# Low parts of the up projection's weights: from VectorE's subtractions to accumulating transfers

## What is computed

```python
kernel = 2.0 * einsum('hn,hnl->hl', Cs, exp(P)).real      # one filter of 1024 taps per channel h
y = irfft(rfft(u * mask) * rfft(kernel))[..., :L] + u * mask * D
y = y * mask
# y as rows of 1024 (xf), 64 batches x 64 channels
scores = xf @ Wr.T                                        # 64 experts
top_vals, top_idx = top_k(scores, 16); gates = softmax(top_vals)
h = einsum('nd,krd->nkr', xf, A)                          # up: 1024 -> 64 experts x 16
out = einsum('nkr,kdr->nd', h * G[:, :, None], B) * 2.0   # down: 64 x 16 -> 1024
return x + out
```

## Time and profile before

| what | value |
|---|---|
| median of the runs | 894.25 us |
| the profiled execution | 894.25 us, its span 892.5 us |
| TensorE busy | 879.5 us, 99% of the span |
| VectorE busy | 753.8 us, 84% |
| ScalarE busy | 376.1 us, 42% |
| GpSimd busy | 6.5 us |
| DMA engines, mean busy share by slice of 22.3 us | 0.7, 0.7, 0.2, 0.1, 0.3, 0.1, then about 0.4 |
| one step of the loop | 26.7 us |

### The profile page before, as it was taken

How to read it: one execution, slowest core, us unless ns; L and a number is a source line. 1 busy time by engine, 2 the same in 40 slices (tenths; PEclk the granted TensorE clock), 3 DMA queues, 4 the chain that set the end, 5 groups by cost and what they waited for, 6 DMA issues and landing times.

```text
span 892.5 us, 15771 instructions
## 1 busy us (share of the span) xinstructions
PE 879.5 (99%) x4478; PEld 781.4 (88%) x4478; DVE 753.8 (84%) x2597; ACT 376.1 (42%) x642; POOL 6.5 (1%) x22
## 2 busy tenths in 40 slices
PE   5999999999999999999999999999999999999998
PEld 3667999998889998889999889999889999889997
DVE  8989998988889888889888889888889888888722
ACT  5763563444444344444344444334444334442100
POOL 2000000000000000000000000000000000000000
PEclk9999999999999999999999999999999999999999
DMA  7721315444333444333444434444333445333331
GB/s 238 241 57 47 77 33 141 141 118 121 115 120 108 124 118 126 115 119 111 118 118 131 113 117 110 118 118 137 110 116 108 118 118 141 111 114 114 93 95 48
DMA packets 74759, 103.32 MB, mean 116 GB/s; under 512 B 23972, under 2 KB 56804, under 8 KB 74740
## 3 DMA queue, kind: packets, MB, share of 16 engines
q1 hardware_dynamic: 74212, 102.63, 40.2%
q0 software_dynamic: 160, 0.10, 0.2%
q10 hardware_dynamic: 368, 0.36, 0.1%
HBM read 67.34 MB, written 34.93 MB: 115 GB/s over the span
## 4 chain that ended last, share of the span: by engine, by line
PE 95%; DVE 3%; ACT 1%; issue 0%; DMA 0%; ACTq 0%; DVEq 0%
PE out_ps L1432 26%; PE h_ps L1432 19%; PE out_ps L1436 13%; PE h_ps L1436 9%; PE turn_ps L1432 8%; PE turn_ps L1436 4%; PE conv_ps L1388 2%; PE conv_ps L1389 2%; PE conv_ps L1390 2%; PE conv_ps L1361 1%; PE conv_ps L1398 1%; PE conv_ps L1362 1%; PE conv_ps L1399 1%; PE conv_ps L1400 1%; PE conv_ps L1363 1%; PE h_ps L1441 1%
## 5 line engine op out<-in xcount | busy, mean ns | idle before, releaser
L1432 PE MATMUL out_ps<-b_lo,g_hi 128*128 128x512 f32 x496 | 196.1, 395 | 0.0
L1432 PE MATMUL out_ps<-b_hi,g_hi 128*128 128x512 f32 x496 | 194.7, 393 | 0.3 <-ACT g_hi L584 0.3
L1432 PE MATMUL h_ps<-a_hi,y_hi 128*128 128x384 f32 x480 | 161.4, 336 | 0.0
L1432 PE MATMUL h_ps<-a_lo,y_hi 128*128 128x384 f32 x480 | 161.3, 336 | 0.0
L1436 PE MATMUL out_ps<-b_hi,g_lo 128*128 128x512 f32 x496 | 122.6, 389 | 0.0
L1432 PEld LDWEIGHTS out_ps<-b_lo,g_hi 128*128 128x128 f32 x496 | 93.2, 188 | 21.2
L1432 PEld LDWEIGHTS out_ps<-b_hi,g_hi 128*128 128x128 f32 x496 | 93.0, 188 | 20.4 <-ACT g_hi L584 0.9
L1436 PEld LDWEIGHTS out_ps<-b_hi,g_lo 128*128 128x128 f32 x496 | 93.0, 188 | 20.0
L857 DVE SCALAR_TENSOR_TENSOR z<-swapped,step_other,part 128x64 f32<-128x64 f32 x384 | 92.3, 282 | 11.9
L850 DVE SCALAR_TENSOR_TENSOR part<-z,step_own,conv_ps 128x64 f32<-128x64 f32 x384 | 90.5, 277 | 8.7 <-ACT z L486 0.4
L1436 PE MATMUL h_ps<-a_hi,y_lo 128*128 128x384 f32 x480 | 93.1, 336 | 0.0
(11 more groups left out here) (244 smaller groups left out, 1480.7 us busy)
## 6 DMA issues: line engine op xcount, KB each, us to landing
xt_in<-in_xt SPq DMA_DIRECT2D x32, 512.0 KB, 3.3
x_in<-in_x SPq DMA_DIRECT2D x62, 256.0 KB, 3.7
out<-x_in SPq DMA_DIRECT2D x62, 256.0 KB, 3.1
moved<-square_sb SPq DMA_DIRECT2D x28, 512.0 KB, 2.7
square_sb<-moved SPq DMA_DIRECT2D x112, 128.0 KB, 2.9
b_in<-in_b_t SPq DMA_DIRECT2D x8, 512.0 KB, 7.8
a_in<-in_a_t SPq DMA_DIRECT2D x8, 512.0 KB, 9.1
moved_in<-square_in SPq DMA_DIRECT2D x26, 128.0 KB, 2.8
```

Source lines behind the costliest of these rows:

```text
L1432: pe.matmul(o, hi[:, c, :], moving[:, c, columns], start=first and c == order[0] and moving is w_hi, stop=False)
```

## The change

`low_up` is gone from VectorE. ScalarE writes the negative of the rounded high part over `a_in` (which is `a_lo`'s memory) in three calls, each for one third, and GpSimd issues transfers that add `a_t` and `wr_t` from memory to it: -a_hi + a = a_lo. The order is part 2, part 0 (two transfers), part 1. Part 2's columns are turned before tile 1 has used them, so tile 1's last third is multiplied from high and low parts; for that tile 1's `y` gets a high part (ScalarE) and a low part (VectorE), and the last four chunks of `a`'s columns 0 to 384 are rounded early in one call (`high_last`), the rest of these chunks in `split_rest`.

```diff
@@ gpsimd @@
+            pool.wait_ge(s_minus_hi, 1)
+            pool.dma_start(a_lo[:, :, 0:384], a_t[:, :, 0:384], accum_op=ALU.add).then_inc(s_alo[2], 16)
+            pool.wait_ge(s_minus_hi, 2)
+            pool.dma_start(a_lo[:, :, 768:ER], a_t[:, :, 768:ER], accum_op=ALU.add).then_inc(s_alo[0], 16)
+            pool.dma_start(a_lo[:, :, ER:EW], wr_t, accum_op=ALU.add).then_inc(s_alo[0], 16)
+            pool.wait_ge(s_minus_hi, 3)
+            pool.dma_start(a_lo[:, :, 384:768], a_t[:, :, 384:768], accum_op=ALU.add).then_inc(s_alo[1], 16)
@@ scalar @@
+            def high_last():
+
+                for i in LATE[5:]:
+                    act.wait_ge(s_w[i], 16)
+                act.activation(a_hi[:, NC // 2:NC, 0:384], a_in[:, NC // 2:NC, 0:384], ACT.Copy).then_inc(s_hilast, 1)
+
+            def split_rest(i):
+
+                _, arrived, hi, _ = loads[i]
+                act.activation(hi[:, 384:ER], arrived[:, 384:ER], ACT.Copy).then_inc(s_whi, 1)
+
+            def minus_high(n, up_before, highs):
+
+                _, c0, width, _ = H_PARTS[n]
+                act.wait_ge(s_up, up_before)
+                act.wait_ge(s_hilast, 1)
+                act.wait_ge(s_whi, highs)
+                act.activation(a_lo[:, :, c0:c0 + width], a_in[:, :, c0:c0 + width], ACT.Copy, scale=-1.0).then_inc(s_minus_hi, 1)
@@ scalar, first_step @@
                 decays(2)
+                high_last()
+                minus_high(2, 3, len(HIGH) - 4)
                 sines(2)
...
                 first_copies(2)
+                for i in range(HT):
+                    high_y(1, i)
                 tables(3)
                 for i in LATE[5:]:
-                    split_weights(i)
+                    split_rest(i)
@@ scalar, second_step @@
                 high_z(2)
+                minus_high(0, 4, len(HIGH))
                 high_turned(1, 0, 2, g_hi)
...
                 high_x(3)
+                minus_high(1, 5, len(HIGH))
                 copy_k(3)
@@ vector @@
-            def low_up(n):
-
-                _, c0, width, _ = H_PARTS[n]
-                columns = slice(c0, c0 + width)
-                dve.wait_ge(s_whi, len(HIGH))
-                dve.wait_ge(s_up, 3 + n + 1)
-                dve.tensor_tensor(out=a_lo[:, :, columns], in0=a_in[:, :, columns], in1=a_hi[:, :, columns].bitcast(F32),
-                                  op=ALU.subtract).then_inc(s_wlo, 1)
@@ vector, second_step @@
                 gate(1)
+
+                for i in range(HT):
+                    low_y(1, i)
                 states(2, range(MIDDLE, FED))
                 gates_of(1)
                 gate_part(1, 0)
-                low_up(0)
                 low_near(2)
...
-                low_up(1)
                 for i in range(HT):
                     low_y(2, i)
                 low_x(3)
-                low_up(2)
@@ tensor, up @@
-                    if first:
-                        pe.wait_ge(s_wlo, len(MIDST) + n + 1)
+                    if first and n < 2:
+                        pe.wait_ge(s_whi, len(HIGH))
+                        pe.wait_ge(s_alo[n], 16 * (2 - n))
@@ tensor, second_step @@
-                for n in range(len(H_PARTS)):
+                for n in range(2):
                     for c in range(NC):
                         last = whole_product(n, c)
                     last.then_inc(s_up, 1)
+
+                o, c0, width, _ = H_PARTS[2]
+                pe.wait_ge(s_yhi, HT)
+                pe.wait_ge(s_alo[2], 16)
+                product_high(o, y_hi, a_hi, a_lo, slice(c0, c0 + width), range(NC), first=True)
+                pe.wait_ge(s_ylo, HT)
+                product_low(o, y_lo, a_hi, slice(c0, c0 + width), range(NC)).then_inc(s_up, 1)
```

More of the change, by code:

```diff
@@ L207, in build @@
         s_whi, s_wlo = sem("s_whi"), sem("s_wlo")
+        s_hilast, s_minus_hi, s_alo = sem("s_hilast"), sem("s_minus_hi"), [sem(f"s_alo_{n}") for n in range(3)]
         s_theta, s_whole, s_args, s_sine, s_decay, s_powers, s_other, s_raw = (
@@ L878, in low_y @@
                 head = slice(i * B, (i + 1) * B)
-                dve.wait_ge(s_yhi, HT * (t - EXACT) + i + 1)
+                dve.wait_ge(s_yhi, HT * (t + 1 - EXACT) + i + 1)
                 dve.tensor_tensor(out=y_lo[:, :, head], in0=y_m[:, :, head], in1=y_hi[:, :, head].bitcast(F32),
                                   op=ALU.subtract).then_inc(s_ylo, 1)
-            def low_up(n):
-                _, c0, width, _ = H_PARTS[n]
-                columns = slice(c0, c0 + width)
-                dve.wait_ge(s_whi, len(HIGH))
-                dve.wait_ge(s_up, 3 + n + 1)
-                dve.tensor_tensor(out=a_lo[:, :, columns], in0=a_in[:, :, columns], in1=a_hi[:, :, columns].bitcast(F32),
-                                  op=ALU.subtract).then_inc(s_wlo, 1)
             def low_weights(i):
@@ L1451, in up @@
                     if n == 0:
-                        pe.wait_ge(s_ylo, HT * (t - EXACT) + HT)
+                        pe.wait_ge(s_ylo, HT * (t + 1 - EXACT) + HT)
                     product_low(o, y_lo, a_hi, slice(c0, c0 + width), range(NC)).then_inc(s_up, 1)
@@ L1549, in third_step @@
                 pe.wait_ge(s_glo, 4)
-                pe.wait_ge(s_yhi, HT)
+                pe.wait_ge(s_yhi, 2 * HT)
                 up(2, True, first=True)
@@ L1567, in step @@
                 pe.wait_ge(s_hg, 3 * t)
-                pe.wait_ge(s_yhi, HT * (t - EXACT) + HT)
+                pe.wait_ge(s_yhi, HT * (t + 1 - EXACT) + HT)
                 up(t, conv)
```

## The result

The changed kernel took 909.23 us, the median of 6 runs (907.5 to 913.33), against 894.2 us for the kernel before (893.94 to 894.29, 6 runs): a ratio of 1.0175, with a 95% interval of 1.0154 to 1.0196. It is slower, as forecast, but by 15.0 us instead of 4.2, and outside the range of 893.2 to 902.5. The profiled execution of after has a span of 907.7 us, 15.2 more than before. The six runs spread with the clock that TensorE was granted on the mean: 0.994 in the shortest, 0.988 in the longest.

The account below looks back on a forecast made before the run. The prediction took TensorE as the bound, busy 879.5 of 892.5 us. Its terms, -1.0 + 1.4 + 3.8 = +4.2 us on 894.25, gave 898.5 us, with a range of 893.2 to 902.5 that left out the slow case.

Parts of the forecast that it names:

- place one: Tile 2's x (xt_in) meets the first accumulate on the DMA engines: 1.4 us of new TensorE wait at feed(2).
- the first third: Tile 2's first third: its accumulated data land by 86 us and are asked for at 88.9, so no wait.
- The factor behind it: An accumulate reads its destination as well as its source, so it was priced at twice a plain copy.
- the sign: Profile check number 5: the accumulates take 9 to 12 us from issue to landing.
- The rival of copy price: Accumulates cost only a copy, 4.5 us; the collision with tile 2's x remains: 894.6 us, chance 0.22.
- if the two queues alternate packet by packet: Sharing between tile 2's xt_in and the first accumulate: 1.1 us delay if alternating, 1.6 if sharing time evenly; 1.4 taken.
- slow transfers: Rival: accumulates cost three times a copy, adding waits of 1.8 and 13.4 us at tile 2's thirds: 909.9 us, chance 0.20.
- second reading: With sixteen pieces in a packet, the engines would keep xt_in back until the accumulate is over.
- Place two: Tile 2's second (middle) third: TensorE asks at 92.4 us for the third accumulate's data and waits 3.8 us.
- I take the middle: The wait at tile 2's middle third set at 3.8 us, between 1.6 undisturbed and 5.9 with queueing.
- Gain: 1.00 us, all on the path: Tile 1's last third takes 4.16 us instead of 5.16 on TensorE, and all of that shortens the kernel.
- everything hidden: Rival: xt_in is not delayed and the last accumulate lands in time, leaving only the 1.0 us gain: 893.25 us, chance 0.12.

Follow-up runs that it names:

- a4_plain: The changed kernel with its four accumulating transfers made plain, without the addition, so the output differs: 906.49 us, ratio 1.0141.
- c1_with_x: The changed kernel, but VectorE again subtracts the middle third's low part, and the first accumulate waits for the event releasing tile 2's x: 893.86 us, 0.9992.
- b1_warm: The changed kernel with 20 useless matmuls ahead of feed(2) and 34 ahead of tile 2's middle third: 905.67 us, ratio 1.0129.
- d1: c2_all_with_x with ScalarE's third negative put ahead of high_x(3) instead of behind it: 900.2 us, ratio 1.0065.
- d2: d1 with SyncE's store of tile 1 also held until the last accumulate has landed: 899.09 us, ratio 1.0057.
- e1_near_first: c1_with_x with low_near moved ahead of gates_of in each step on VectorE: 893.77 us, ratio 0.9992.
- a1_wait_x: The changed kernel with the first accumulate issued only when tile 2's x has landed: 909.94 us, ratio 1.0175.
- a3_both: The changed kernel with a1_wait_x's wait, and the middle third's low part made by VectorE's subtraction again: 895.56 us, ratio 1.0015.
- b3_split: The changed kernel with only part 2 accumulated, in two halves, the second once tile 2's x has landed; VectorE makes parts 0 and 1: 896.23 us, 1.0019.
- c2_all_with_x: The changed kernel with all four accumulates, the first waiting for the event that releases tile 2's x: 902.25 us, ratio 1.0102.

## Why the prediction was right or wrong

**Right.** The gain on TensorE's list is 1.00 us to the digit. L889 is gone, the sines start at 51.65, and no run shows TensorE waiting for ScalarE's new work at place one. The two places are the right two, and the first third is in time. The engine time of an accumulate was well forecast: the 27.5 us taken for the four transfers are 107 ns for the mean of 256 packets, and after has (3.4% - 0.2% for q0's other work) of 907.7 us on 16 engines over 4160 packets, 112 ns. The factor behind it was less right. The plain transfers of a4_plain take 73 ns by the same reckoning (2.3% of 904.9), so these plain transfers cost more than the copies in the earlier trace rows (whether for the queue or because they write float32r isn't tested), and with the addition they cost 1.5 times as much as without. From issue to landing the sign was 9 to 12 us; two of the four took longer, 13.6 and 15.4. The half rate that the Trainium skill gives for a reduce ("Collectives: The Full Stack", section "The bandwidth ceiling: the fold count and why AG ≠ RS ≠ AR") is the upper side of that. The rival of copy price has fallen, and a4_plain shows that it would have saved only 2.7 us.

**Wrong, place one: 1.4 us taken, 4.66 measured.** The failing step is "if the two queues alternate packet by packet: 1.1 us; if they share the time evenly: 1.6". It took the sharing to begin with SyncE's first packet. The views show even sharing only from 55.9 on; ahead of that nothing of `xt_in` moves for about 3 us. c1_with_x, with the same accumulate issued 2.8 us later, has none of this. The prediction had it in words, under slow transfers ("a queue that keeps SyncE's transfers back until its own is over"), and bound it to a price three times a copy. a4_plain shows that the two are not bound. The second reading that I gave the Trainium skill's rule on queues ("DMA: Bandwidth & Descriptors", section "Queues, rings and completion order"), many pieces in a packet, isn't borne out as such: `xt_in` starts long before GpSimd's transfer ends. A smaller error: the first accumulate's data start 2.3 us after its issue (49.67 to 52.0), not 0.9 as for SyncE's.

**Wrong, TensorE's clock: 0 taken, 4.8 measured.** The sum had no term for what a wait does to the matmuls behind it. Before has no long wait after 57 us, so no row showed it; but the term was put at nothing without a reason. b1_warm shows that the cost hangs on TensorE's idle time.

**Place two: 3.8 us taken, 6.25 measured,** just above the upper end of 5.9. Everything there is 5.69 + 1.00 = 6.69 us late by place one. Without that the third accumulate is issued at 83.2 (forecast 83.4), lands 15.4 us later at 98.6 (forecast 98.3) and TensorE asks at 92.4, as forecast. So the sum for the upper end was right to 0.3 us, and the step that failed is "I take the middle": the queueing that made up the upper end did happen, behind the earlier accumulates and beside SyncE's transfers. d1 and d2 name two parts of the wait, 2.3 us and 1.3 us. The single terms don't all match: t_lo and the store were put at 3.3 us, and holding the store back gains 1.3.

**"Gain: 1.00 us, all on the path" is in doubt,** though nothing in after shows it. The loop step in the earlier trace rows has TensorE busy throughout, and I took this for room on the other engines. The traces of c1_with_x and e1_near_first show that in the steps before it VectorE lies less than 1 us behind: a TensorE that comes early waits. Whether the rival "everything hidden" would have kept its whole 1.0 us stays open: c1_with_x, its nearest case, has 0.05 us left at 188 us in its trace, which is of its slowest run, while its median is 0.9992 of before with an interval that holds 0.9989, the value of 893.25.

**The sum.** 3.3 us of the miss are place one, 4.8 the clock, 2.4 place two and 0.5 later steps: together the 11.0 us between the forecast of 4.2 and 15.2. The range failed with them. The slow rival's 909.9 lies near the result by chance: its price, three times a copy, and its waits at place two didn't come true. It had been left out of the range.

**What stays open.** Why SyncE's packets are held when GpSimd's data already flow isn't settled. Counted from 0.9 us after their issue they were held about 3 us in after and a4_plain, 3.3 in a1_wait_x, nearly 4 in a3_both and about 1.1 in b3_split, where the earlier transfer had all but run out by then. The runs exclude the addition as the cause, and a fixed count of packets.

## What to carry to other kernels

Before moving work from an engine to a large background transfer, list the small transfers without slack that are issued while it runs, and let those go first: here one added wait moved the kernel with c1_with_x's remaining accumulates from 900.8 to 893.9 us, and making the transfers cheaper hardly did. Price a TensorE wait of several microseconds as its length and, on top, a stretch at half clock behind it: here 1.8 to 2.8 us behind the waits of 4.6 us and more, while behind the one of 3.2 us the clock stayed at 1.00. And before a microsecond taken from the busiest engine is counted as gained, look how far behind the next engine in the loop is: here VectorE was less than that behind.

## What the runs showed of the hardware

- A transfer from GpSimd's queue that adds to its destination: 1.5 MB in 1024 pieces of 1536 bytes lands 12.9 to 14.7 us after its issue as the first accumulate and 14.4 to 17.0 us as the third; without the addition 10.2 and 11.2 us. Half of it takes 8 us.
- A SyncE transfer of 512 KB lands 3.3 us after its issue when alone, 8.1 and 7.9 us when it is issued 2.2 and 2.4 us behind such a transfer, and 8.2 us at 2.2 us behind a plain one. Issued 1.0 and 1.1 us behind an accumulate (after, c2_all_with_x) it takes 4.6 and 4.2 us; its data then begin first, and the accumulate's 3.8 and 3.6 us after their own issue.
- TensorE at the 1.2 GHz level after waits of 4.9 and 6.3 us, and 2.0 and 2.8 us lost to it; with useless matmuls in both waits the granted clock stayed at 1.00.
- Pairs of small VectorE operations (`z`) at 2.7 to 3.1 us instead of 0.48 while GpSimd subtracts, and pairs of `part` at their usual 0.47; GpSimd needs 1.8 us for 128 x 768.
